# The second layer's experts in a two-layer kernel: four dense experts against tokens sent to their two experts in 35 tiles of 128 slots

## The chip, the cores and the metric

The kernel runs on one core of one Trainium2 chip. The metric is the device time of one execution in microseconds (us), as the median of several runs. Engines are called TensorE (PE in the rows, PEld for its weight loads), VectorE (DVE), ScalarE (ACT), GpSimd (POOL) and SyncE (SP); a "q" behind a name means what the engine's sequencer issues, such as DMA.

## The reference

Two layers work on x of shape (2, 1024, 128), all in float32. Each layer adds a gated attention and then a gated expert network, each of them on a normalised x. The change concerns the second layer's expert network and where its routing is worked out:

```python
logits = xf @ gate_w.T                       # 8 experts, of which the last 4 are masked out
weights = softmax(logits)
top_w, top_idx = top_k(weights, 2)
top_w = top_w / sum(top_w)                   # cw: the two weights of a token, zero elsewhere
h = silu(einsum('td,edh->teh', xf, w1)) * einsum('td,edh->teh', xf, w3)    # h is 704 wide
y = einsum('teh,ehd->ted', h, w2)
out = einsum('te,ted->td', cw, y)
x = x + gb * out
```

There are 2048 tokens, four live experts, and every token uses two of them. The attention before it is a linear attention with 16 heads of 32 and decay 0.99, written in chunks of 128 tokens. The first layer has an RWKV-style scan and 16 experts, of which each token uses one.

## The kernel before

The program is a row of phases, each with an instruction stream per engine, ordered by hand with semaphores: set-up, the first layer's scan (`rwkv_phase`), its experts (`expert_phase`), the second layer's attention (`hla_phase`) and its experts (`swiglu_phase`). The weights of the second layer are loaded during the scan.

The first layer's experts already work by dispatch, and are of use as a model. GpSimd scatters the 16 tiles of token rows into slots in DRAM with an indirect transfer each (L1012). SyncE reads from a list in SBUF which expert each tile of 128 slots has (`value_load`, eight at the head of each round), loads the weights (L971) and the rows (L975). The results go back through DRAM, and GpSimd gathers them (L1019). TensorE's matmuls there have fixed addresses.

The attention (`hla_phase`) takes, for each of the 8 chunks, 8 units (2 batches by 4 groups of 4 heads), one a step, so 64 steps and a few more to fill and drain. Steps are pipelined: step k projects unit k+2 (L1325 to L1327), transposes and multiplies k+1 (L1340, L1341, L1363), and finishes k and k-2 (L1383 to L1426). VectorE has three instructions a step: the decay on the chunk's matrix (L1498), the state (L1501) and the masking of 128x1536 products (L1507), for which TensorE waits at the next step's products. Twice a chunk the output projection runs (L1350), ScalarE copies it (L1474), and GpSimd scales it and adds it to x (L1523, L1526). The first and the last chunk are written out; the six between are a loop, so TensorE returns to the loop's head five times.

The experts (`swiglu_phase`) begin when all of x is there. A prologue normalises the 16 tiles (L1730 to L1742, L1799, L1801), transposes them (L1630), works out logits (L1624), the top two and a table of weights per token and expert. Then four groups of 512 tokens run through all four experts. GpSimd multiplies the rows by each expert's weight (L1813), TensorE transposes them (L1647), and each of 22 units per group (a slice of 128 of the hidden width) has two up matmuls of 512 columns with the weights as the stationary side (L1661, the tails in L1663), a silu on ScalarE (L1718), a product on VectorE (L1786) and a down matmul into one accumulator (L1671). Every f32 matmul shows as two instructions, a transpose as one. At a group's end the output is transposed back (L1690), gated (L1790), added to x (L1829) and stored by SyncE (L1837).

## Time and profile before

| | |
|---|---|
| median of three runs | 977.8 us (977.65 to 982.03) |
| the profiled execution, its time | 981.48 us |
| its span in the profile | 979.7 us |
| TensorE busy with matmuls | 778.6 us, 79% of the span |
| VectorE, ScalarE, GpSimd busy | 418.8, 296.4 and 185.3 us |
| mean granted TensorE clock | 0.852 of full speed |

Busy time of an engine is the time in which at least one of its instructions runs. Matmuls are pipelined, so a matmul's own duration is longer than its pitch (the distance between starts), and the pitch is what counts in a stream. A granted clock of 1.00 is 2.4 GHz, of 0.50 is 1.2 GHz. An idle time in brackets stands before an instruction, with what ended it; "issue" means that nothing seen in the profile did.

### The profile page before, as it was taken

The page shows a single profiled execution, that of the slowest core. Times are in us where ns is not written, and L with a number is a line of the kernel's source. Part 1 is how long each engine was busy: PE and PEld are TensorE (multiplying, and loading weights), DVE is VectorE, ACT ScalarE, POOL GpSimd, SP SyncE. Part 2 cuts the span into 40 slices and gives each one's busy share as a digit, 9 for nine tenths or more (in the row PEclk, how much of TensorE's full clock was granted, in tenths as well). Part 3 has the DMA queues.
Part 4 walks back from the last instruction along what each step waited for, and adds up shares of the span by engine and source line. Part 5 has one row for each costly group of instructions (what it writes and reads, how often), then busy time and mean ns, then how long its engine had stood idle before and what let it go on. Part 6 is the DMA issues. An engine that isn't in the chain of part 4 may idle for free. (4 is left out here: it accounts for less than half of the span.)

```text
span 979.7 us, 25889 instructions
## 1 busy us (share of the span) xinstructions
PE 778.6 (79%) x10310; PEld 544.4 (56%) x10310; DVE 418.8 (43%) x1142; ACT 296.4 (30%) x903; POOL 185.3 (19%) x285
## 2 busy tenths in 40 slices
PE   3777777754238608998898988999459999999997
PEld 3455555533238506887787877887334444444442
DVE  4367777772413264444443444444522222222221
ACT  0243333330014304443333433343122222222221
POOL 1244444432230170000000000000221010110100
PEclk9587777765559858999999999999659999999999
DMA  4600000002147510000000000000000000000000
GB/s 139 220 3 2 0 0 0 0 2 86 34 144 232 156 38 2 4 3 4 3 4 3 3 4 3 4 3 3 1 0 1 0 12 0 11 0 0 11 0 11
DMA packets 27297, 28.11 MB, mean 29 GB/s; under 512 B 3201, under 2 KB 20289, under 8 KB 27201
## 3 DMA queue, kind: packets, MB, share of 16 engines
q1 hardware_dynamic: 26176, 24.58, 8.1%
q0 software_dynamic: 1024, 2.10, 0.7%
q8 instruction: 79, 1.29, 0.6%
q14 instruction: 18, 0.14, 0.0%
HBM read 20.38 MB, written 6.29 MB: 27 GB/s over the span
## 5 line engine op out<-in xcount | busy, mean ns | idle before, releaser
L1507 DVE TENSOR_TENSOR h_masked<-quad,const 128x1536 f32<-128x1536 f32 (+2 forms) x66 | 112.8, 1709 | 143.3 <-PE quad L1369 136.5
L1661 PE MATMUL quad<-f_xg,moe_w 128*128 128x512 f32 x320 | 152.3, 601 | 0.8 <-ACT f_xg L1706 0.8
L1786 DVE TENSOR_TENSOR f_h<-f_sa,quad 128x512 f32<-128x512 f32 x88 | 60.6, 688 | 181.0 <-PE quad L1661 164.6
L1661 PEld LDWEIGHTS quad<-f_xg,moe_w 128*128 128x128 f32 x320 | 60.2, 193 | 69.8 <-issue 69.1
L1718 ACT ACTIVATE f_sa<-quad 128x512 f32<-128x512 f32 x88 | 52.5, 597 | 143.7 <-PE quad L1661 126.6
L1671 PE MATMUL bank<-f_h,moe_w 128*128 128x512 f32 x160 | 82.5, 597 | 0.0
L1523 POOL TENSOR_TENSOR h_added<-h_added,mod_row 128x128 f32<-128x128 f32 x16 | 7.3, 455 | 285.2 <-ACT h_added L1474 285.2
L1671 PEld LDWEIGHTS bank<-f_h,moe_w 128*128 128x128 f32 x160 | 29.7, 190 | 40.9 <-issue 40.9
L1478 ACT ACTIVATE h_gT<-bank 128x128 f32<-128x128 f32 x64 | 17.7, 277 | 113.4 <-PE bank L1412 111.9
L1363 PE MATMUL quad<-h_qk 32*128 32x128 f32 x1024 | 49.6, 311 | 0.0
L1325 PE MATMUL pair<-h_hT,hla_wq 128*128 128x128 f32 x128 | 32.1, 334 | 20.4 <-issue 16.6
L1454 ACT ACTIVATE h_qk<-pair 128x256 f32<-128x256 f32 x64 | 24.5, 383 | 71.6 <-PE pair L1327 71.6
L1363 PEld LDWEIGHTS quad<-h_qk 32*128 32x128 f32 x1024 | 36.8, 197 | 10.8 <-issue 8.8
L633 POOL TENSOR_TENSOR kl<-kl,tot 128x128 f32<-128x128 f32 x56 | 26.9, 481 | 60.7 <-DVE tot L543 28.7
L1813 POOL TENSOR_TENSOR g_hs<-g_h_all,g_cw 128x512 f32 (+1 forms) x20 | 20.6, 1040 | 93.0 <-PE pair L1647 71.6
L1829 POOL TENSOR_TENSOR x_sb<-x_sb,f_gated 128x512 f32 x4 | 5.1, 1266 | 155.9 <-DVE f_gated L1790 155.9
L1325 PEld LDWEIGHTS pair<-h_hT,hla_wq 128*128 128x128 f32 x128 | 19.6, 193 | 24.8 <-issue 18.3
L1498 DVE TENSOR_TENSOR h_aT<-bank,const 128x128 f32<-128x128 f32 x64 | 18.7, 292 | 30.1 <-PE bank L1426 27.4
L711 ACT ACTIVATE rl<-rl 128x128 f32<-128x128 f32 x56 | 17.3, 308 | 44.6 <-DVE rl L544 28.4
L1383 PE MATMUL bank<-h_qk,h_state 32*32 32x128 f32 x512 | 28.1, 290 | 0.0
L757 PE MATMUL quad<-lh,b_pad 128*128 128x256 f32 x64 | 27.2, 598 | 0.7 <-ACT lh L666 0.7
L1019 POOL DMA_INDIRECT e_yt<-slots_out,slot_of_token x16 | 15.7, 978 | 62.8 <-DMA slots_out<-e_yg 58.3
(287 smaller groups left out, 1685.8 us busy)
## 6 DMA issues: line engine op xcount, KB each, us to landing
e_w<-in_experts_dram SPq DMA_DIRECT2D x32, 257.5 KB
moe_w<-in_moe_w_dram SPq DMA_DIRECT2D x2, 1408.0 KB, 9.2
slots_in<-zero SPq DMA_DIRECT2D x4, 512.0 KB, 4.0
e_xg<-slots_in SPq DMA_DIRECT2D x8, 256.0 KB, 3.0
slots_out<-e_yg SPq DMA_DIRECT2D x8, 256.0 KB, 4.8
moe_w<-in_moe_w_dram SPq DMA_DIRECT2D x4, 320.0 KB, 7.0
x_sb<-in_L_attn_x_dram SPq DMA_DIRECT2D x2, 512.0 KB, 8.5
out_dram<-x_sb SPq DMA_DIRECT2D x4, 256.0 KB, 2.3
```

What stands on the lines that cost most here:

```text
L633: pool.tensor_tensor(halves(kl[m + 1], m)[:, :, 0], halves(kl[m], m)[:, :, 0], per(tot[m], m)[:, :, 1:2].to_broadcast([P, N >> (m + 1), 1 ...
L757: mm = pe.matmul(bank[2 + f // 2][:, f % 2 * N:(f % 2 + 1) * N], b_pad[:, f, :], lh[:, :], start=True, stop=True)
L1325: pe.matmul(proj[:, 0:P], W["q"][:, cols], hT[b][:, :], start=True, stop=True)
L1363: last = pe.matmul(quad[:, h, a * P:(a + 1) * P], qk[q][head(h), 1 - a, :], qk[q][head(h), a, :], start=True, stop=True, tile_position=(h ...
L1383: pe.matmul(left[head(h), 0:P], states[k][head(h), 2 * D:3 * D], qk[k][head(h), 1, :], start=True, stop=False, tile_position=(h * D, h * D ...
L1454: act.activation(qk[q][:, :, :], proj[:, 0:2 * P].rearrange("p (k n) -> p k n", k=2), ACT.Copy).then_inc(s_qkv, 1)
L1507: dve.tensor_tensor(masked[k % 4][:, :, a * P:z * P], quad[:, :, a * P:z * P], cst("causal")[:, None, a * P:z * P].to_broadcast([P, HPG, ( ...
L1661: return pe.matmul(dst[:, :], w[:, e, f * P:(f + 1) * P], src(e), start=True, stop=True)
L1671: pe.matmul(acc[b][:, :], w, hh[n % 2][:, :], start=(n == 0), stop=(n == U - 1))\
L1718: act.activation(sa[n % 2][:, :], up_a[n % 2][:, :], ACT.Silu).then_inc(s_sa, 1)
L1786: dve.tensor_tensor(hh[n % 2][:, :], sa[n % 2][:, :], up_b[n % 2][:, :], ALU.mult)\
L1813: pool.tensor_tensor(hs[k % 2][:, :, :], h_all[:, bass.ds(at + k, 1), :].to_broadcast([P, E, C]), cw[:, 0, bass.ds(at + k, 1), :].rearrang ...
```

## The change

The two phases become one, `layer1_phase`. Four things change.

1. **Routing during the attention.** As soon as a chunk's x is there, the steps of the next two chunks carry its routing: statistics (step 3), centring (4), normalising (5), logits as products on GpSimd and sums on VectorE (7), the top two (0), ranks by two small matmuls on TensorE (1), slots and weights (2). The attention's second chunk is now written out too, so the loop has five turns and four returns.
2. **Dispatch.** A payload row has 132 numbers: the normalised row, the token's number, its weight and its batch. GpSimd sends each tile's rows to the slots of its first and of its second expert: four indirect transfers a chunk. The slots in DRAM are filled with blank rows during the scan. SyncE writes x into an accumulator in DRAM as it becomes ready.
3. **The expert loop.** 35 tiles of 128 slots (the most that four experts can need), in 7 rounds of 5, the last one written out. TensorE reads from SBUF which expert each tile has, six `value_load`s at a round's head (five in the last), and takes the weights by that register. Now the tokens are the stationary side and the weights move: three up matmuls of 512, 512 and 384 columns hold w1 and w3 side by side, the hidden tile is transposed (4 + 2 transposes) and six down matmuls of 128 columns make the rows. One tile's parts are interleaved with the next one's.
4. **Results.** VectorE multiplies a row by weight and gate, and GpSimd adds the tile into the accumulator with an accumulating indirect transfer, each after the one before has landed, since two tiles can hold the same token. At the end SyncE copies the accumulator, 1 MB, from DRAM to the output.

```diff
+CAP1 = BATCH * SEQ
+TILES1 = 2 * BATCH * SEQ // P + E1_LIVE - 1
+SLOTS1 = E1_LIVE * CAP1 + (E1_LIVE - 1) * P
+PAY = C + 4
+S_W2 = 7 + E1_LIVE
...
+        W2 = {"up": sb("moe_up", [P, E1_LIVE, 2 * F1]), "w2": sb("moe_w2", [P, E1_LIVE, FULL1, C]),
+              "w2_tail": sb("moe_w2_tail", [TAIL1, E1_LIVE, C])}
+        blank = sb("blank", [P, PAY])
+        s_fill = sem("s_fill1")
+        t["moe1_slots"] = nc.dram_tensor("moe1_slots", (SLOTS1, PAY), F32, kind="Internal").ap()
+        t["moe1_acc"] = nc.dram_tensor("moe1_acc", (BATCH * SEQ + P, C), F32, kind="Internal").ap()
...
-                hla_phase(nc, x_bc, mod_row, quad, bank, pair, cst, hT_all, W1, s_w1)
-        with nc.cleanup_on_exit():
-            swiglu_phase(nc, t, x_sb, eps_pow, sbw[:, 1], mod_row, bank, pair, cst, W2, s_w2, out)
+                layer1_phase(nc, t, x_sb, x_bc, eps_pow, sbw[:, 1], mod_row, quad, bank, pair, cst, hT_all, W1, s_w1,
+                             W2, s_w2, s_fill, blank, out)
...
+            sp.dma_start(t["moe1_slots"].rearrange("(q p) n -> p q n", p=P),
+                         blank[:, None, :].to_broadcast([P, SLOTS1 // P, PAY])).then_inc(s_fill, 16)
...
+            for i in range(2):
                 for k in range(PER):
-                    step(n + 1, k)
+                    step(i, k)
+            with eng.Fori(0, CHUNKS - 3) as n:
+                for k in range(PER):
+                    step(n + 2, k)
...
+        def routed(i, k, at):
+            if k % PER != at:
+                return None
+            m = i + k // PER - (1 if at >= 3 else 2)
+            return m if not isinstance(m, int) or m >= 0 else None
...
+            pe.wait_ge(s_gate, 16)
+            for e in range(E):
+                last = pe.matmul(left[:, e * C:(e + 1) * C], gate[:, e:e + 1].to_broadcast([P, P]), cst("ident"),
+                                 start=True, stop=True)
+            last.then_inc(s_grow, 1)
+            pe.wait_ge(s_growc, 1)
...
+            def rank(m, first):
+                pe.wait_ge(r_ohs, m + 1)
+                pe.wait_ge(r_cum, m * 2 + 1)
+                pe.nop(nofuse=True)
+                pe.matmul(right[:, 232:240], cst("before"), ohs[:, :, :].rearrange("p b e -> p (b e)"), start=first,
+                          stop=False, skip_group_check=True)
+                pe.matmul(right[:, 232:240], cst("ones"), cum[:, :, :].rearrange("p b e -> p (b e)"), start=False,
+                          stop=True, skip_group_check=True).then_inc(r_rank, 1)
...
+            def ups(i, k, u, e):
+                if u == 0:
+                    pe.wait_ge(f_xT, tile(i, k) + 1)
+                pe.wait_ge(f_hh, tile(i, k) * 3 + (u + 1))
+                pe.nop(nofuse=True)
+                w = 2 * WIDTH[u]
+                pe.matmul(up[u][:, 0:w], xT[k][:, :],
+                          W2["up"][:, bass.ds(e, 1), u * 4 * P:u * 4 * P + w].rearrange("p e n -> p (e n)"),
+                          start=True, stop=True).then_inc(f_up, 1)
+            def turn_most(i, k):
+                pe.wait_ge(f_hh, tile(i, k) * 3 + 5)
+                pe.wait_ge(f_mostc, tile(i, k) + 1)
+                for f in range(4):
+                    last = pe.transpose(most[:, f * P:(f + 1) * P], hh[k][:, f * P:(f + 1) * P], cst("ident"))
+                last.then_inc(f_most, 1)
+            def turn_rest(i, k):
+                pe.wait_ge(f_hh, tile(i, k) * 3 + 6)
+                pe.wait_ge(f_restc, tile(i, k) + 1)
+                for f in range(2):
+                    last = pe.transpose(rest[:, f * P:(f + 1) * P], hh[k][:, (4 + f) * P:(5 + f) * P], cst("ident"))
+                last.then_inc(f_rest, 1)
+            def down(i, k, e):
+                pe.wait_ge(f_mostc, tile(i, k) + 2)
+                pe.wait_ge(f_restc, tile(i, k) + 2)
+                pe.wait_ge(f_y, tile(i, k) + (1 if k else 2))
+                pe.nop(nofuse=True)
+                for f in range(FULL1):
+                    pe.matmul(acc[k % 2], hidT[k][:, f * P:(f + 1) * P],
+                              W2["w2"][:, bass.ds(e, 1), f, :].rearrange("p e n -> p (e n)"), start=(f == 0),
+                              stop=False)
+                pe.matmul(acc[k % 2], hidT[k][0:TAIL1, FULL1 * P:(FULL1 + 1) * P],
+                          W2["w2_tail"][:, bass.ds(e, 1), :].rearrange("p e n -> p (e n)"), start=False,
+                          stop=True).then_inc(f_down, 1)
+            def expert(n):
+                return pe.value_load(expert_of[0:1, bass.ds(n, 1)], min_val=0, max_val=E - 1)
+            def round_(i, last):
+                es = [expert(tile(i, k)) for k in range(U if last else U + 1)]
+                for k in R:
+                    j, q = (i, k + 1) if k + 1 < U else (i + 1, 0)
+                    more = not last or k + 1 < U
+                    ups(i, k, 2, es[k])
+                    turn_most(i, k)
+                    if not last or k + 2 < U:
+                        turn(*((i, k + 2) if k + 2 < U else (i + 1, k + 2 - U)))
+                    if more:
+                        ups(j, q, 0, es[k + 1])
+                    turn_rest(i, k)
+                    if more:
+                        ups(j, q, 1, es[k + 1])
+                    down(i, k, es[k])
+            turn(0, 0)
+            first = expert(0)
+            ups(0, 0, 0, first)
+            turn(0, 1)
+            ups(0, 0, 1, first)
+            with pe.Fori(0, ROUNDS - 1) as i:
+                round_(i, False)
+            round_(ROUNDS - 1, True)
...
+            def weigh(m):
+                act.wait_ge(r_gap, m + 1)
+                act.activation(eg[:, :], gap[:, :], ACT.Exp).then_inc(r_eg, 1)
...
+            def top2(m):
+                dve.wait_ge(r_lg, m * 2 + 2)
+                dve.nop(nofuse=True)
+                for b in range(BATCH):
+                    dve.max(mx[:, b, :], lg[:, b, :]).then_inc(r_mx, 1)
+                dve.wait_ge(r_mx, m * 2 + 2)
+                dve.nop(nofuse=True)
+                for b in range(BATCH):
+                    dve.max_index(idx[:, b, :], mx[:, b, :], lg[:, b, :]).then_inc(r_idx, 1)
+                dve.tensor_tensor(gap[:, :], mx[:, :, 1], mx[:, :, 0], ALU.subtract).then_inc(r_gap, 1)
+                dve.wait_ge(r_idx, m * 2 + 2)
+                dve.tensor_copy(idf[:, :, :], idx[:, :, 0:2]).then_inc(r_idf, 1)
+                dve.wait_ge(r_idf, m + 1)
+                dve.tensor_tensor(oh[:, :, :, :],
+                                  cst("iota16")[:, None, None, 0:E].to_broadcast([P, BATCH, 2, E]),
+                                  idf[:, :, :, None].to_broadcast([P, BATCH, 2, E]), ALU.is_equal).then_inc(r_oh, 1)
+                dve.wait_ge(r_oh, m + 1)
+                dve.tensor_tensor(ohs[:, :, :], oh[:, :, 0, :], oh[:, :, 1, :], ALU.add).then_inc(r_ohs, 1)
+                dve.wait_ge(r_ohs, m + 1)
+                dve.tensor_tensor(cum[:, 1, :], cum[:, 0, :], ohs[:, 0, :], ALU.add).then_inc(r_cum, 1)
...
+                m = routed(i, k, 2)
+                if m is not None:
+                    ranked(m)
                 if live(i, k, -3, LAST):
                     q = unit(i, k, -3)[1]
                     dve.scalar_tensor_tensor(out=states[q][:, :], in0=states[q][:, :], scalar=GAMMA ** P,
                                              in1=right[:, P:P + 3 * D], op0=ALU.mult, op1=ALU.add).then_inc(s_st, 1)
+                if m is not None:
+                    slots(m)
+                    weights(m)
+                for at, part in ((3, stats), (4, centre), (5, normalise), (7, logits), (0, top2)):
+                    m = routed(i, k, at)
+                    if m is not None:
+                        part(m)
...
+            def hidden(i, k, u):
+                dve.wait_ge(f_sa, (i * U + k) * 3 + (u + 1))
+                at, w = u * 2 * P, WIDTH[u]
+                dve.tensor_tensor(hh[k][:, at:at + w], sa[u][:, 0:w], up[u][:, w:2 * w], ALU.mult).then_inc(f_hh, 1)
+            def keep_rest(i, k):
+                dve.wait_ge(f_rest, i * U + (k + 1))
+                dve.tensor_copy(hidT[k][:, 4 * P:6 * P], rest).then_inc(f_restc, 1)
+            def result(i, k):
+                n = i * U + (k + 1)
+                dve.wait_ge(f_down, n)
+                dve.wait_ge(f_gs, n * 3)
+                if not isinstance(i, int) or i:
+                    dve.wait_ge(f_add, (i * U + (k + 1 - U)) * 16 + 16)
+                dve.scalar_tensor_tensor(out=yg[k][:, :], in0=acc[k % 2], scalar=xg[k][:, C + 1:C + 2],
+                                         in1=gsel[k][:, :], op0=ALU.mult, op1=ALU.mult).then_inc(f_y, 1)
+            def round_(i, last):
+                for k in R:
+                    hidden(i, k, 2)
+                    j, q = (i, k + 1) if k + 1 < U else (i + 1, 0)
+                    keep_rest(i, k)
+                    if not last or k + 1 < U:
+                        hidden(j, q, 0)
+                        hidden(j, q, 1)
+                    result(i, k)
...
+            def chunk(i, first=2, last=False):
+                if first >= 1:
+                    add(i - 1, 1)
+                if not last:
+                    pool.wait_ge(s_proj, i * PER + GROUPS)
+                    fetch(i + 1, 0)
+                if first >= 2:
+                    send(i - 2)
+                if first >= 1:
+                    deviation(i - 1)
+                    products(i - 1)
+                    payload(i - 1)
+                add(i, 0)
+                if not last:
+                    pool.wait_ge(s_proj, i * PER + 2 * GROUPS)
+                    fetch(i + 1, 1)
+            chunk(0, 0)
+            chunk(1, 1)
+            with pool.Fori(0, CHUNKS - 3) as n:
+                chunk(n + 2)
+            z = CHUNKS - 1
+            chunk(z, 2, True)
+            send(z - 1)
+            add(z, 1)
+            deviation(z)
+            payload(z)
+            send(z)
+            pool.wait_ge(r_sent, CHUNKS * 64)
+            pool.wait_ge(s_acc, 16 * TILES)
+            pool.wait_ge(s_table, 1)
...
+            def send(m):
+                pool.wait_ge(r_pay, m * 2 + 2)
+                pool.wait_ge(r_slot, m + 1)
+                pool.wait_ge(r_cw, m * 3 + 3)
+                pool.nop(nofuse=True)
+                for b in range(BATCH):
+                    for k in range(2):
+                        pool.indirect_dma_start(out=t["moe1_slots"], out_offset=bass.IndirectOffsetOnAxis(
+                            ap=slot[:, b * 2 + k:b * 2 + k + 1], axis=0), in_=pay[:, b, k, :], in_offset=None)\
+                            .then_inc(r_sent, 16)
...
+            def select(i, k):
+                pool.wait_ge(f_x[k], i * 16 + 16)
+                pool.nop(nofuse=True)
+                pool.tensor_copy(token_of[k][:, :], xg[k][:, C:C + 1]).then_inc(f_gs, 1)
+                pool.tensor_tensor(gsel[k][:, :], gdiff[:, :], xg[k][:, C + 2:C + 3].to_broadcast([P, C]),
+                                   ALU.mult).then_inc(f_gs, 1)
+                pool.wait_ge(f_gs, (i * U + k) * 3 + 2)
+                pool.tensor_tensor(gsel[k][:, :], gsel[k][:, :], mod_row[:, 1, 1, 0, :], ALU.add).then_inc(f_gs, 1)
+            def scatter(i, k):
+                n = i * U + (k + 1)
+                pool.wait_ge(f_gs, n * 3)
+                pool.wait_ge(f_y, n + 2)
+                pool.wait_ge(f_add, n * 16)
+                pool.nop(nofuse=True)
+                pool.indirect_dma_start(out=t["moe1_acc"], out_offset=bass.IndirectOffsetOnAxis(
+                    ap=token_of[k][:, 0:1], axis=0), in_=yg[k][:, :], in_offset=None, compute_op=ALU.add)\
+                    .then_inc(f_add, 16)
             with pool.Fori(0, ROUNDS) as i:
-                for b in range(BATCH):
-                    prepare(*following(i, b))
-                    pool.wait_ge(s_gated, group(i, b) + 3)
-                    xs = x_sb[:, bass.ds(i * TPG + b * CHUNKS, TPG), :]
-                    pool.tensor_tensor(xs, xs, gated[b][:, :, :], ALU.add).then_inc(s_x, 1)
+                for k in R:
+                    select(i, k)
+                    scatter(i, k)
+            pool.wait_ge(f_add, 16 * TILES1 + 16)
...
+            def rows_of(i):
+                return [sp.value_load(row_of[0:1, bass.ds(i * U + k, 1)], min_val=0, max_val=SLOTS1 - P) for k in R]
+            def load(k, row):
+                sp.dma_start(xg[k][:, :], t["moe1_slots"][bass.ds(row, P), :]).then_inc(f_x[k], 16)
+            for k, row in enumerate(rows_of(0)):
+                load(k, row)
+            with sp.Fori(0, ROUNDS - 1) as i:
+                following = rows_of(i + 1)
+                for k in R:
+                    sp.wait_ge(f_y, i * U + (k + 3))
+                    sp.nop(nofuse=True)
+                    load(k, following[k])
+            sp.wait_ge(f_add, 16 * TILES1 + 16)
+            whole = "(q r) n -> q (r n)"
+            sp.dma_start(out.rearrange("b s n -> (b s) n").rearrange(whole, q=P),
+                         t["moe1_acc"][0:BATCH * SEQ, :].rearrange(whole, q=P)).then_inc(f_out, 16)
+            sp.wait_ge(f_out, 16)
```

Not shown are the new constants, the layout of the weight loads (w1 and w3 in six transfers side by side), VectorE's table of 35 tiles worked out on one partition after the last chunk, and the small bodies of `stats`, `centre`, `normalise`, `logits`, `ranked`, `slots`, `weights` (13 VectorE instructions a chunk), `deviation`, `products` and `payload` (six on GpSimd), of which `products` has two of 128x512. ScalarE's and VectorE's waits in the expert loop follow TensorE's order.

## Rows read from the trace of the kernel before

**Rows 1.** Busy time by stretch: length, each engine (instructions), granted clock, DMA share, GB/s.

```profile
370.80:691.00 320.20, 298.35 (x7232) 259.65 (x7232) 141.20 (x194) 120.78 (x464) 21.62 (x48) 0.96 0.01 3
691.00:728.60 37.60, 14.63 (x64) 12.69 (x64) 18.55 (x124) 6.40 (x11) 11.30 (x15) 0.52 0.01 1
728.60:972.40 243.80, 241.52 (x636) 105.19 (x636) 62.63 (x91) 66.36 (x109) 20.91 (x22) 0.99 0.01 4
```

**Rows 2.** Timeline of TensorE in the expert loop: start us, us, engine, line, what.

```profile
746.15 1.88 PE L1661 MATMUL quad<-f_xg,moe_w 128*128 128x512 f32 x4
...
747.87 1.02 PE L1671 MATMUL bank<-f_h,moe_w 128*128 128x512 f32 x2
```

**Rows 3.** Timeline of TensorE in the first layer's experts, 128-column matmuls.

```profile
319.75 0.39 PE L1212 MATMUL bank<-const,e_w 128*128 128x128 f32 x2
319.97 0.61 PE L1209 MATMUL bank<-e_w,e_hid 128*128 128x128 f32 x4
```

**Rows 4.** Timeline of TensorE in an attention step, transposes.

```profile
588.02 0.27 PE L1341 MATMUL pair<-const,h_qk 128*128 128x128 f32 x1
588.12 0.27 PE L1345 MATMUL pair<-const,h_gT 128*128 128x128 f32 x1
```

**Rows 5.** Costliest groups, VectorE and ScalarE: busy and mean ns | idle before.

```profile
L1786 DVE TENSOR_TENSOR f_h<-f_sa,quad 128x512 f32<-128x512 f32 x88 | 60.6, 688 | 181.0 <-PE quad L1661 164.6
...
L1718 ACT ACTIVATE f_sa<-quad 128x512 f32<-128x512 f32 x88 | 52.5, 597 | 143.7 <-PE quad L1661 126.6
```

**Rows 6.** Timeline of VectorE and SyncE around the first layer's register loads.

```profile
260.91 0.17 DVE L1109 TENSOR_SCALAR expert_of_tile<-r_te 1x32 int32<-1x32 f32 x1
...
266.16 4.36 SPq L971 DMA_DIRECT2D e_w<-in_experts_dram  x8
...
298.35 0.41 SPq L979 DMA_DIRECT2D slots_out<-e_yg  x1
...
304.70 0.39 SPq L975 DMA_DIRECT2D e_xg<-slots_in  x1
```

**Rows 7.** Timeline of TensorE at a return of the attention loop.

```profile
449.54 0.48 PE L1325 MATMUL pair<-h_hT,hla_wq 128*128 128x128 f32 x2 [3.05 <-issue]
```

**Rows 8.** Busy time by stretch around the same return.

```profile
448.00:450.00 2.00, 0.46 (x4) 0.47 (x5) 0.00 (x0) 0.00 (x0) 0.00 (x0) 1.00 0.00 0
450.00:452.00 2.00, 2.00 (x20) 1.67 (x22) 0.00 (x0) 1.33 (x5) 0.00 (x0) 0.54 0.03 8
```

**Rows 9.** Timeline of ScalarE, the copy that comes twice a chunk.

```profile
421.94 0.38 ACT L1474 ACTIVATE h_added<-pair,const 128x128 f32<-128x128 f32 x1
...
439.88 0.38 ACT L1474 ACTIVATE h_added<-pair,const 128x128 f32<-128x128 f32 x1
...
462.48 0.38 ACT L1474 ACTIVATE h_added<-pair,const 128x128 f32<-128x128 f32 x1
```

**Rows 10.** Timeline of GpSimd and SyncE, last scatter and the load after it.

```profile
279.77 0.95 POOL L1012 DMA_INDIRECT slots_in<-h_all,slot_of_token  x1 [0.31 <-issue]
...
282.01 0.94 SPq L975 DMA_DIRECT2D e_xg<-slots_in  x2
```

**Rows 11.** DMA issues: count, KB each, median us from issue to landing.

```profile
e_xg<-slots_in SPq DMA_DIRECT2D x8, 256.0 KB, 3.0
...
x_sb<-in_L_attn_x_dram SPq DMA_DIRECT2D x2, 512.0 KB, 8.5
...
e_yt<-slots_out,slot_of_token POOLq DMA_INDIRECT x16, 2.5
...
g_gate<-in_gate_cols_dram SPq DMA_DIRECT2D x1, 2.0 KB, 1.6
```

**Rows 12.** Timeline of an attention step, VectorE and TensorE's next products.

```profile
589.35 1.76 DVE L1507 TENSOR_TENSOR h_masked<-quad,const 128x1536 f32<-128x1536 f32 x1 [1.61 <-PE quad L1369]
...
592.59 0.73 PE L1363 MATMUL quad<-h_qk 32*128 32x128 f32 x16
```

**Rows 13.** Timeline of GpSimd, the last addition to x.

```profile
690.30 0.45 POOL L1526 TENSOR_TENSOR x_sb<-x_sb,h_added 128x128 f32<-128x128 f32 x1
```

551 lines of the change are left out of this document (282 added, 269 removed).

## The prediction

> **What bounds the kernel now.** I read first the busy time by stage. The second layer's attention runs from 370.8 to 691.0 us and its experts from 728.6 to 972.4 us, with a routing prologue of 37.6 us between. In both long stages TensorE is busy nearly throughout (298 of 320 us, 241.5 of 243.8 us), and no other engine reaches half the stage [rows 1]. So an instruction added to another engine costs nothing while it fits beside TensorE, and whatever shortens or stretches TensorE's stream moves the end. Second, the timeline gives the pitch of that stream: four passes of 512 columns take 1.72 us, 0.43 us each, two to a matmul [rows 2]; an f32 matmul of 128 columns takes 0.22 us (two passes) [rows 3], a transpose 0.10 us, say 0.11 [rows 4]. Third, I looked at what happens when TensorE's sequencer has nothing to hand over, at a loop's return and at register loads, since the new loop has these.
>
> **The expert loop.** Removed: 243.8 us. Each of 35 tiles has three up matmuls (512, 512 and 384 columns: 0.86 + 0.86 + 0.65 = 2.37), seven transposes (0.77) and six down matmuls (1.32): 4.46 us. That is 156 us in all; the halved count of experts is partly spent on transposes and on 35 tiles where 32 would be full. I take 4.6 us for small gaps at the four no-operations that wait. Do the others keep up? ScalarE has three silus and two copies: an activation or copy of 256 columns is near 0.4 us and one of 512 is 0.60 on the rows of VectorE and ScalarE scale [rows 5], in all about 2.0 us; VectorE has three products, a copy and the result, about 1.7. Both are below half, and each hand-over (silu, product, back to a transpose) has an up matmul of 0.86 us over it. So they cost nothing; without that cover each hand-over would show about 1 us.
>
> Every matmul on the experts' weights now takes its address from a register. No TensorE row shows one. Below: nothing (SyncE's register-addressed loads already go out at 4.36 / 8 = 0.55 us, near the 0.39 of an ordinary issue). Above: 0.15 us for each of nine, 1.4 us a tile, 47 us. A dispatch of this size hides under passes of 0.43 us, so I take nothing and keep 20 us for the range.
>
> **Register loads, at every round's head.** TensorE reads six expert numbers into registers before each round of five tiles. SyncE shows what such a load costs: the expert list is written at 261.1, and the first weight load goes out at 266.16, after eight of them: 0.63 each. In the loop, 298.76 to 304.70 is 5.94 for eight, 0.74 each with the loop's return [rows 6]. Six cost 3.8 to 4.4 us; the matmuls already handed over (the last down group, 1.32 us) cover about 0.9. I take a hole of 3.5 us. The nearest TensorE row is the attention loop's own return: idle 3.05 us before the first matmul of a turn [rows 7], and then a stretch at a granted clock of 0.54, which is the 1.2 GHz level against 1.00 before [rows 8]. Its whole price is that a half chunk takes 22.60 instead of 17.94 us: 4.66 [rows 9]. So each hole is 3.5 + 1.3 = 4.8 us, six of them 29 us. Bounds: nothing, if TensorE's loads are quick; 6 us each if they also wait for the array. In the Trainium skill, "DMA: Bandwidth & Descriptors", section "Latency and other measured facts", a tensor load has a floor of about 600 ns; by it the six would take 3.6 us, 0.2 us less a hole than by the rows. The Trainium skill, "TensorE: Matmul & The Clock Gate", section "HAM oscillation", adds that a loop which stops between bursts of matmuls is throttled again in each turn; that speaks against this change, and rows 8 agree at a hole of this size. Were the clock to hold, the six holes would cost 21 us.
>
> So the loop is 35 x 4.6 = 161, less 1.7 (no next tile in the last one), plus 29, plus 1.3 for a cold start: 189.6 us.
>
> **The scatter-add.** GpSimd sends each tile's rows with an accumulating indirect transfer, and each waits for the one before to land. The nearest row is a plain scatter: issued at 279.77, all landed when SyncE moves at 282.01, 2.24 us [rows 10]. If the read of the old rows adds a whole gather (2.5 us [rows 11]), that is 4.7, about 5 with the wait. GpSimd's own work (select about 1.4, issue 0.95 + 0.31 = 1.26 [rows 10]) fits in 2.8. A round averages 5.56 us a tile (4.6 plus 4.8 / 5), and results are five deep. I take 3.5 us and no cost; it begins to cost at 5.56. The row loads (3.0 us to land [rows 11]) are issued three tiles ahead, 9 us of cover.
>
> **The attention stage.** Moved in: statistics, normalising, logits, top two, ranks, slots and sends, one or two parts per step. TensorE's added work is two tiny matmuls per chunk, 0.22 each, with waits about 0.6: 7 x 0.6 = 4 us. VectorE has in each step 1.61 us idle before the big masking product [rows 12], and TensorE wants that product about 1.5 us after its end, so 3 us fit into a step. The largest part (top two, ten small instructions of about 0.2) is 1.8, logits 1.4. Queued behind them is only the mask. GpSimd's four sends per chunk take 4 x 1.26 = 5 us of a half chunk, and the normalising that waits for them comes two steps later. So no stall; without this cover 1 to 2 us per chunk, up to 15. One chunk more is written outside the loop: one return less, -4.7. Ahead of the stage, loading gate rows (1.6 us to land, four matmuls, a copy) delays TensorE by 3.5. The last steps lose 1. Sum +4.
>
> **Between attention and loop.** The send of chunk 6 now stands on GpSimd ahead of the last addition, which ended at 690.75 [rows 13]: four issues, +4.6. The last x is ready at 690.75 + 4 + 4.6 = 699.4. From there: statistics 0.9, deviation 1.2, normalising 0.6, products 1.4 (VectorE 0.69 each [rows 5]), logits 1.4, top two 1.5, ranks 0.9, slots and weights 1.4: 9.3. Then four sends and their landing, 6.3; SyncE's five register loads 3.1 and the first row load 2.9; transpose and copy 0.9; and before the loop's first instruction the first six register loads, of which 4.8 us count. Sum 27.3. The loop begins at 726.7, where its predecessor began at 728.6: the removed 37.6 us are spent again on latency.
>
> **The tail.** Before, 972.4 to 979.7, 7.3 us. Now: result 0.5, last scatter about 3.5, and a DRAM to DRAM copy of 1 MB, nearest row 8.5 us for 1 MB in two loads at the start [rows 11]; I take 7.5 with its issue, 0.9 to the end: 12.4. Bounds 8 and 16.
>
> **Sum.** 726.7 + 189.6 + 12.4 = 928.7, against 979.7: 51 us less. The profiled execution took 981.5 us, 1.8 outside the span and 3.7 above the median of 977.8; 977.8 - 51 = **927 us**.
>
> **Rivals.** (a) TensorE's register loads hide under queued matmuls or are quick. Against: SyncE's rows; for: no TensorE row. Loop -29, start -4: 894 us. (b) Tiles of 5.2 to 5.8 us, by register addresses or hand-overs that miss their cover: +21 to +42, 948 to 969. (c) The routing work in the attention stalls TensorE, by a late send or mask: +15 to +30, 942 to 957. (d) The other side: the serial chain of scatter-adds sets the pace. It costs from 5.56 us a link, equals the time before at 5.56 + 51 / 35 = 7.0, and at 8 us a link gives 927 + 35 x 2.44 = 1012. For it: each transfer waits for the last, and no row shows an accumulating one; against: the plain scatter lands in 2.24 us.
>
> **How the numbers follow.** Forecast 0.53 (910 to 942), (a) 0.17, (b) 0.14, (c) 0.07, (d) 0.09, of which 0.06 is slower. The predicted time is that of the forecast, 927. The range 888 to 965 takes in (a) and most of (b) and (c). A measurement tells about 0.5% (5 us): faster 0.92, same 0.02, slower 0.06.
>
> **What would show it.** Right: seven holes of 3 to 4 us on TensorE at the rounds' heads, with the granted clock near 0.5 behind each; a pitch near 4.6 us within a round; attention steps of unchanged length; first up matmul near 722. Wrong: GpSimd's scatter waiting for the transfer before it while TensorE waits for VectorE's result; masking products that start late in the steps with logits or top two; holes missing.

## The result, and the profile after

The changed kernel takes **1000.4 us** (median of 4, 997.9 to 1004.1), the kernel before 979.9 beside it: ratio 1.021, 95% interval 1.016 to 1.026. So it is slower, by about 2%; 927 us was forecast, range 888 to 965. The profiled execution has a span of 1002.3 us.

The same marks that the forecast was built on, in us from the start of the span:

| mark | before | forecast | after | added to the miss |
|---|---|---|---|---|
| last row of the first layer's scan (ScalarE, zT) | 229.5 | 229.5 | 239.8 | +10.3 |
| first half-chunk copy of the attention (ScalarE, h_added) | 404.0 | 407.5 | 420.3 | +2.5 |
| last half-chunk copy | 689.3 | 693.3 | 751.1 | +45.0 |
| last addition to x ends | 690.8 | 699.4 | 757.9 | +0.7 |
| first up matmul | | 721.9 | 780.8 | +0.4 |
| last down matmul ends | 972.4 | 916.3 | 990.9 | +15.7 |
| end of the span | 979.7 | 928.7 | 1002.3 | -1.0 |

Busy time by stretch of the changed kernel (length, PE, PEld, DVE, ACT and POOL busy with counts, granted clock, DMA share, GB/s); it answers to [rows 1]:

```profile
383.60:752.00 368.40, 327.84 (x7268) 279.24 (x7268) 174.59 (x382) 129.13 (x477) 73.62 (x114) 0.91 0.04 10
752.00:780.70 28.70, 2.06 (x7) 1.61 (x7) 9.81 (x48) 1.97 (x4) 11.98 (x17) 0.53 0.11 31
780.70:991.00 210.30, 184.15 (x874) 117.87 (x874) 65.56 (x175) 64.99 (x174) 88.23 (x137) 0.94 0.16 21
991.00:1002.30 11.30, 0.00 (x0) 0.00 (x0) 0.27 (x1) 0.00 (x0) 1.58 (x1) 0.58 0.33 99
```

The expert loop did become shorter, 210 us for 244. But the attention, whose matmuls are the same but for two small ones a chunk, went from 320 to 368 us. TensorE idles 40.6 us of it for 21.9, and the granted clock is 0.91 for 0.96. No other engine is near full there either. So the stage didn't get a new bound; it got holes. The list of TensorE's waits in that stage says of which kind (engine, tile, line <- what ended the wait: us in total, times, longest):

```profile
PE pair L1430 <- issue: 16.1, 5, 3.6
PE pair L1431 <- issue: 10.1, 4, 2.7
PE bank L1494 <- issue: 6.4, 11, 1.0
PE bank L1488 <- issue: 4.8, 14, 0.4
PE bank L1409 <- DMA g_gate<-in_gate_cols_dram: 3.5, 1, 3.5
```

No wait for a mask, a rank or a send is among them. "Issue" is a wait for nothing that the profile shows. Before, the only wait for issue was the one of the first line (16.6 us, 5 times). Three places are to be seen. First, a return of the loop, timeline of TensorE, answering to [rows 7]:

```profile
504.06 0.24 PE L1546 MATMUL bank<-h_vt,h_kqt 128*32 128x32 f32 x8
507.87 0.50 PE L1430 MATMUL pair<-h_hT,hla_wq 128*128 128x128 f32 x2 [3.56 <-issue]
511.02 0.79 PE L1431 MATMUL pair<-h_hT,hla_wk 128*128 128x128 f32 x2 [2.65 <-issue]
```

There is a second stop of 2.65 us after the first two matmuls of a turn, where [rows 7] had one stop and then went on. Second, the half chunk in which GpSimd issues its four sends (527.0 to 531.9), TensorE and GpSimd:

```profile
529.67 0.96 POOL L1978 DMA_INDIRECT moe_slots<-g_pay,g_slot  x1 [0.30 <-issue]
529.73 0.37 PE L1488 MATMUL bank<-h_qk,h_state 32*32 32x128 f32 x2 [0.34 <-issue]
...
530.47 0.42 PE L1488 MATMUL bank<-h_qk,h_state 32*32 32x128 f32 x5 [0.36 <-issue]
...
530.94 0.96 POOL L1978 DMA_INDIRECT moe_slots<-g_pay,g_slot  x1 [0.30 <-issue]
531.18 0.27 PE L1488 MATMUL bank<-h_qk,h_state 32*32 32x128 f32 x1 [0.29 <-issue]
```

and the stretches around it:

```profile
528.00:530.00 2.00, 1.66 (x29) 1.21 (x26) 1.09 (x6) 0.00 (x0) 1.39 (x3) 1.00 0.20 57
530.00:532.00 2.00, 1.01 (x11) 0.42 (x11) 0.00 (x0) 1.34 (x5) 1.62 (x3) 1.00 0.17 53
532.00:534.00 2.00, 1.54 (x21) 1.08 (x20) 1.15 (x1) 0.00 (x0) 0.91 (x2) 0.52 0.10 34
534.00:536.00 2.00, 2.00 (x42) 1.77 (x44) 0.61 (x1) 0.32 (x2) 0.00 (x0) 0.50 0.00 0
```

I call it the stutter: TensorE gets its matmuls in crumbs for some 4 us, of which it idles about 1.8, and the granted clock then falls from 1.00 to 0.50 (1.2 GHz) for some 7 more (it is 0.77 in 538 to 540 us and 1.00 from 540 on). What both cost is read from ScalarE's copy, as in [rows 9]:

```profile
497.70 0.38 ACT L1685 ACTIVATE h_added<-pair,const 128x128 f32<-128x128 f32 x1
...
524.69 0.38 ACT L1685 ACTIVATE h_added<-pair,const 128x128 f32<-128x128 f32 x1
...
548.89 0.38 ACT L1685 ACTIVATE h_added<-pair,const 128x128 f32<-128x128 f32 x1
```

The half chunk with the return takes 26.99 us (22.60 before), the one with the sends 24.20 (17.94 before). Third, the scan, which the change doesn't touch. At 51.4 us TensorE stops 2.0 us before line 820, and where the kernel before has its clock back at about 51 us (0.92 in 50 to 55 us, 1.00 in 55 to 60), this one stays at the half level until 68 us:

```profile
50.00:55.00 5.00, 3.56 (x36) 2.88 (x37) 2.16 (x8) 1.02 (x4) 1.26 (x3) 0.50 1.23 274
55.00:60.00 5.00, 5.00 (x31) 2.73 (x30) 1.95 (x4) 0.00 (x0) 2.58 (x5) 0.50 0.30 67
```

The 274 GB/s are the fill of the slot rows, which is new.

In the expert loop, the end of a round and the head of the next, timeline of TensorE:

```profile
809.11 1.34 PE L1618 MATMUL bank<-moe_w,h_masked 128*128 x10
810.39 0.48 PE L1621 MATMUL bank<-moe_w_tail,h_masked 64*128 x2
815.19 1.46 PE L1594 MATMUL quad<-moe_up,f_xT 128*128 x2 [4.31 <-issue]
```

The holes forecast at 3.5 us are there, with 4.1 to 4.3 us at five heads of rounds and 2.6 at the last, which has five loads and no return. At the first of the seven heads TensorE idles only 1.43 us. The pitch inside a round is 4.925 us (the tail's down matmul starts at 790.69, 795.61, 800.54, 805.46), not 4.6.

### The profile page after: what moved, and what is told of

Same layout as the page of the kernel before. It is cut to its first block, busy times and chain, and to the rows that moved or that the text cites. A ratio compares the mean times of both kernels' runs of the same rounds, so it can differ in the third digit from the quotient of the medians.

```text
span 1002.3 us, 28133 instructions
## 1 busy us (share of the span) xinstructions
PE 747.4 (75%) x10523; PEld 571.3 (57%) x10524; DVE 447.4 (45%) x1347; ACT 298.7 (30%) x974; POOL 307.9 (31%) x473
## 3 DMA queue, kind: packets, MB, share of 16 engines
q8 instruction: 81, 1.33, 0.6%
## 4 chain that ended last, share of the span: by engine, by line
PE 51%; issue 7%; POOL 1%; DMA 1%; DVE 1%; ACT 0%; SPq 0%; POOLq 0%; DVEq 0%; PEldq 0%
PE quad L1594 10%; PE quad L1468 5%; PE bank L1618 4%; PE bank L1494 3%; PE pair L1430 3%; PE bank L1488 3%; PE bank L1521 2%; PE pair L1431 2%; PE quad L1474 2%; PE quad L1602 2%; PE pair L1432 2%; PE bank L1505 2%; PE bank L1538 2%; PE bank L1526 2%; PE bank L1529 2%
## 5 line engine op out<-in xcount | busy, mean ns | idle before, releaser
L1594 PE MATMUL quad<-moe_up,f_xT 128*128 x210 | 111.6, 615 | 25.5 <-issue 23.5
L2045 POOL DMA_INDIRECT moe_acc<-f_y,f_token x35 | 55.4, 1582 | 120.5 <-DVE f_y L1916 120.5
L1904 DVE TENSOR_TENSOR h_masked<-f_sa,quad 128x256 f32<-128x256 f32 (+1 forms) x105 | 41.5, 395 | 85.0 <-ACT f_sa L1713 85.0
L1713 ACT ACTIVATE f_sa<-quad 128x256 f32<-128x256 f32 (+1 forms) x105 | 38.4, 365 | 137.0 <-PE quad L1594 136.2
L1618 PEld LDWEIGHTS bank<-moe_w,h_masked 128*128 128x128 f32 x350 | 41.8, 191 | 22.1 <-issue 22.1
L1594 PEld LDWEIGHTS quad<-moe_up,f_xT 128*128 128x128 f32 x210 | 33.8, 202 | 32.5 <-issue 29.1
L1618 PE MATMUL bank<-moe_w,h_masked 128*128 x350 | 47.0, 281 | 0.7 <-DVE h_masked L1908 0.7
L1430 PE MATMUL pair<-h_hT,hla_wq 128*128 128x128 f32 x128 | 33.7, 348 | 16.9 <-issue 16.1
L1978 POOL DMA_INDIRECT moe_slots<-g_pay,g_slot x32 | 31.9, 997 | 25.9 <-DVE g_pay L1822 16.6
L1494 PE MATMUL bank<-h_aT,h_state 32*32 32x128 f32 x512 | 30.5, 278 | 7.0 <-issue 6.4
L1431 PE MATMUL pair<-h_hT,hla_wk 128*128 128x128 f32 x128 | 27.9, 303 | 10.1 <-issue 10.1
```

Source lines behind the costliest of these rows:

```text
L1430: pe.matmul(proj[:, 0:P], W["q"][:, cols], hT[b][:, :], start=True, stop=True)
L1431: pe.matmul(proj[:, P:2 * P], W["k"][:, cols], hT[b][:, :], start=True, stop=True)
L1494: pe.matmul(left[head(h), P:2 * P], states[q][head(h), part * D:(part + 1) * D], of[head(h), :], start=(part == 2 and not live(i, k, 0)), ...
L1594: pe.matmul(up[u][:, 0:w], xT[k][:, :], W2["up"][:, bass.ds(e, 1), u * 4 * P:u * 4 * P + w].rearrange("p e n -> p (e n)"), start=True, sto ...
L1618: pe.matmul(acc[k % 2], hidT[k][:, f * P:(f + 1) * P], W2["w2"][:, bass.ds(e, 1), f, :].rearrange("p e n -> p (e n)"), start=(f == 0), sto ...
L1713: act.activation(sa[u][:, 0:WIDTH[u]], up[u][:, 0:WIDTH[u]], ACT.Silu).then_inc(f_sa, 1)
```

## The experiments

Times are medians; "before" is the kernel before on the same chip in the same group. It took 980.5, 981.9, 982.8, 980.3 and 980.6 us in the five groups.

### Group 1: four single edits

Fill in the middle of the scan:

```diff
+            sp.wait_ge(s_gT, 5)
+            sp.nop(nofuse=True)
             sp.dma_start(t["moe1_slots"].rearrange("(q p) n -> p q n", p=P), ...
```

> The 4.4 MB fill of the slot rows waits until the scan is at its fifth chunk; nothing else differs from the changed kernel. Theory A (TensorE's instructions arrive late because the fill's transfers, 274 GB/s at 50 us, are ahead of them): the 2.0 us stop before TensorE's line 820 at 51.4 us is gone, the clock rises to 1.00 at about 50 us as before the change (55 to 60 us: 1.00, not 0.50), the last scan row is back from 239.8 near 229.5, and the whole is 8 to 11 us shorter, 990 to 993, unless the fill stops TensorE at its new place. Rival B (the weights, now loaded in 11 transfers with shorter rows in place of 10, or the code's place, are the cause): no change, 1000 to 1003, the stop stays at 51 us.

No sends:

```diff
-                for b in range(BATCH):
-                    for k in range(2):
-                        pool.indirect_dma_start(out=t["moe1_slots"], ...).then_inc(r_sent, 16)
+                pool.sem_inc(r_sent, 64)
```

> GpSimd issues none of the 32 sends (all slot rows keep their blank content, so the experts work on zero rows and add to the spare rows; the output holds x before the experts); routing, masks and rank matmuls stay. Theory A (the sends delay TensorE's instructions): TensorE's waits for issue at lines 1488 and 1494 (4.8 + 6.4 us) are gone, and with them the half clock behind them; the half chunks without a loop return go from 22.8 to 24.2 us back to 17.9 to 18.6, in all 20 to 30 us less, and 5 us less behind the last x where GpSimd is no longer held up; whole about 970 to 978. Rival C (the routing work on VectorE and GpSimd holds TensorE up): 997 to 1003, the half chunks stay. Both: the 3.6 us return and the 2.65 us second stop at lines 1430 and 1431 stay, since no send runs beside them.

x written to the sum table after the attention:

```diff
-            with sp.Fori(0, CHUNKS) as i:
-                for b in range(BATCH): ...
+            for b in range(BATCH):
+                sp.wait_ge(s_x, CHUNKS * BATCH + (b + 1))
+                sp.dma_start(rows[b], x_bc[:, b, :, :]).then_inc(s_acc, 16)
```

> SyncE writes x to the sum table in two transfers of 512 KB when the last x is ready, in place of 16 of 64 KB during the attention. If the 64 KB writes take part in delaying TensorE's instructions (one is issued at 526.5 us, just ahead of the stutter at 528.7 to 533.4): the stutter shrinks by up to half, 5 to 15 us less, 985 to 995. If only the sends do: within 3 us of the changed kernel, 998 to 1003. The two transfers themselves (8.5 us for such a one at the start of the kernel) lie beside the 27 us between the last x and the expert loop; if they don't, up to 5 us more.

TensorE's attention written out:

```diff
-            steps(pe, step)
+            step(0, -2)
+            step(0, -1)
+            for i in range(CHUNKS - 1):
+                for k in range(PER):
+                    step(i, k)
+            for k in range(PER + 3):
+                step(CHUNKS - 1, k)
```

> TensorE's attention steps are written out for all 8 chunks; the other engines keep their loops. The four loop returns of TensorE cost 3.56 + 2.65 us of stop and some 1.7 us at half clock behind each. Theory A (code comes by transfers, a jump back starts them anew): all four stops of both kinds are gone, 4 x (6.2 + 1.7) = 32 us less, about 969; the stutter beside the sends stays. Rival D (the stop at a return is a wait for another engine's return, the loop registers or a barrier of all engines): a stop of 1 to 3.5 us stays at the same place, 985 to 1000. Rival E (written-out code is always fetched too slowly at full rate): the stutter spreads over all chunks, no gain or a loss, 1000 to 1020.

Measured: fill late 963.4 (ratio to before 0.981, 0.976 to 0.986); no sends 960.0; x after 972.4 (0.988, 0.984 to 0.993); written out 936.6 (0.954, 0.949 to 0.960). All gained far more than I gave them against the first run of the changed kernel: the late fill 37 us for 8 to 11, no sends 40 for 22 to 30, x written after 28 for at most 15, written out 64 for 32. In **none** of the four was there a stutter, though three of them send: the half chunks with sends took 17.94 us. That three unrelated edits should each cure it is hard to believe; the next groups have a control. What the group does show: the late fill is 9.0 us below x written after, which has everything else of the changed kernel. With it the stop at line 820 is gone and the clock is 1.00 from 50 us on:

```profile
50.00:55.00 5.00, 5.00 (x39) 3.22 (x38) 3.80 (x12) 1.09 (x5) 3.51 (x7) 1.00 0.00 0
```

and with TensorE written out, all returns with both their stops are gone (last less first half-chunk copy: 264.8 us, where the loop of the kernel before takes 285.3).

### Group 2: a control, two paddings, spread register loads

> The changed kernel once more, word for word, as the control of this group. Three edits that have nothing to do with each other (the fill later, the x rows written later, TensorE's steps written out) each took away the whole stutter of TensorE beside the sends, in two of them with the sends still running. Theory F (the stutter belongs to this one build: where its instructions or rings lie): it is there again, lines 1488 and 1494 wait 11 us for issue, 998 to 1004. Theory G (it belonged to the chip or the moment of the first run): it is gone here, the loop chunk takes 44.5 us in place of 51.2, about 972 (1000 less 5 chunks of some 5 to 6).

Empty instructions on SyncE, and on TensorE:

```diff
+            for n in range(2):
+                sp.nop(nofuse=True)
             for n in "qkv":
                 sp.dma_start(W1[n][:, :], ...
```

> Two empty instructions on SyncE ahead of its weight loads, nothing else, so that later code lies 128 bytes further and nothing that is computed or moved changes. Theory F: if placement decides, the stutter can go: about 972, with the second stop and the fill's 10 us still there; if the edits of the first group took it away by what they do, it stays, 998 to 1004. Theory G: the same time as the control.

```diff
+            for n in range(32):
+                pe.nop(nofuse=True)
             pe.wait_ge(s_gate, 16)
```

> 32 empty instructions on TensorE ahead of the attention, where it waits 3.5 us for the gate columns anyway, so that its loop begins 2 KB later in its code. The second stop (2.65 us after two of the loop's first matmuls, in every return of every kernel that has the loop) is the edge of a block of code right behind the loop's first instructions: moved by 2 KB it is gone and the next block comes while the first runs: 4 x 2.65 = 10.6 us less than the control, and some of the half clock. Rival: the second stop is a property of a return with so many engines in loops: it stays, same time as the control within 3 us.

One register load ahead of each tile (in a round's code on TensorE):

```diff
-                es = [expert(tile(i, k)) for k in range(U if last else U + 1)]
+                es = [expert(tile(i, 0))]
                 for k in R:
...
+                    if more:
+                        es.append(expert(tile(i, k + 1)))
```

> TensorE's register loads of the round's experts stand one ahead of each tile (two ahead of the first) in place of six ahead of the round. If TensorE's matmuls before a load go on while the load is under way (the 1.3 us of downs ahead of it would cover one load of 0.6 to 0.7): 5 holes of 4.2 fall to about 1.5 and the others vanish, 5 x 2.7 + 1.3 of clock each, 15 to 22 us less than the control. If a load stops TensorE fully: the same sum in smaller pieces, each tile some 0.6 longer, and only the half clock behind the long holes is saved: 0 to 8 us less.

Measured: 1000.6, 1003.1, 997.8 and 974.1 us. The stutter is in all four, as in the first run, so the two empty instructions on SyncE do nothing, and the first group's lack of it seems to lie with its chip. The 32 on TensorE left the second stop (2.9 us). The spread loads are worth 26.5 us, more than I expected: the holes, where two loads still stand in a row at a round's head, are 1.3 us at most (6.4 in six), and the tiles between them keep their pitch of 4.92, so a single load that follows 1.3 us of down matmuls is hidden.

### Group 3: the sends and the chip

> The changed kernel once more, as the control of this group. The first group (fill late, no sends, x rows after, TensorE written out) ran on one chip and had no stutter in any kernel; the second (the changed kernel, two kernels with empty instructions, spread loads) ran on another and had it in all four. Theory G (the stutter belongs to the chip): it is in all kernels of this group or in none. Theory A (it belongs to the edit): here and not in the two of this group with the fill late or without sends. Time 998 to 1004 with it, about 970 without.

> The kernel with the fill in the middle of the scan again, beside a control on the same chip. Theory G: the control less 8 to 10 us (the scan's part alone), its stutter as in the control. Theory A: no stutter whatever the control has, 960 to 966, 35 to 40 us below the control. It would mean that a transfer that ended at 56 us decides over TensorE's supply at 500 us, which I hold for unlikely (1 in 4).

> The kernel without the 32 sends again (what it leaves out is as before), beside a control on the same chip. If the control has the stutter and this one not: the sends are one half of its cause, the chip the other; 30 us or more below the control, 957 to 962. If both have it: the sends have no part. If neither has it: this kernel is 5 to 15 us below the control, by the last send that is not waited for.

> Fill in the middle of the scan, TensorE's attention steps written out, register loads spread: the three edits that gained singly (each of them correct). If they add (37 less 28 of stutter, that is 9, and 936.6 for the second, and 26 for the third): 936.6 - 9 - 26 = 902. If the stutter is there on this chip in written-out code too: 25 to 30 more, 925 to 935.

Measured: 1004.4, 996.9, 958.5 and 931.8 us. The control has the stutter, the late fill has it too (so it was never the fill), and the kernel without sends has none. The waits of TensorE there, for issue alone:

```profile
PE pair L1430 <- issue: 16.0, 5, 3.7
PE pair L1431 <- issue: 9.3, 4, 2.7
...
PE pair L820 <- issue: 1.7, 1, 1.7
```

From the first to the last half-chunk copy the control takes 329.7 us and this one 298.5. So on a chip that shows it, the sends cost 31 us of the attention. On the chip of group 1 the nearest pair (fill late with sends, 297.2; fill early without, 298.1) does not differ by more than 1 us. The three edits together (931.8) keep the stutter: written-out code doesn't cure it, the half chunks with sends take 23.0 to 24.3.

The late fill is 7.5 us below its control. The last zT is at 226.3 to 231.7 in the four kernels with the late fill and at 229.9 to 239.8 in all the others of the change, 235 in the mean; so the early fill costs some 2 to 10 us and 6 in the mean, not always the 10.3 of the first profile. These are single executions, and the mark moves by itself: in three profiles of the kernel before and its variants, which have no fill, it is at 227.5, 229.5 and 235.1. The two differences of whole times, 9.0 and 7.5 us, are the better measure.

### Group 4: transfers or their issue; register addresses; before written out

Plain sends, by SyncE:

```diff
+            def sends(m):
+                sp.wait_ge(r_pay, m * 2 + 2)
...
+                        sp.dma_start(t["moe1_slots"][bass.ds(m * 4 * P + (b * 2 + k) * P, P), :], pay[:, b, k, :])\
+                            .then_inc(r_sent, 16)
```

> The 32 sends go as plain transfers of the same 128 rows of 528 bytes, issued by SyncE at the same point of the chunk, to rows that follow each other in place of the routed ones (so the experts work on rows in another order and the sums go wrong); GpSimd issues none. Theory H (the transfers themselves hold up the blocks of TensorE's instructions): the half chunks with sends stay at 22.8 to 24.2 us where the chip shows the stutter at all (see the 12-nop kernel of this group), whole 995 to 1004. Theory I (it is what GpSimd does to issue an indirect send: its descriptors): they fall to 17.9, TensorE waits for issue at lines 1488 and 1494 under 1 us in all, whole 958 to 965.

> 12 empty instructions on TensorE ahead of the attention, 768 bytes of code. With 32 of them (2 KB) the second stop of each loop return stayed at 2.9 us; if it is an edge of a block of 2 KB or a divisor of it that lies 4 to 6 instructions behind the loop's start, 12 move it: the second stop is gone or moved, 10 us less for the stops and up to 10 more for the half clock behind them, 980 to 990. If it stays (2.1 to 2.9 us after the first two matmuls, 996 to 1004), no edge of code explains it. This kernel is also the group's control for the stutter.

Fixed experts:

```diff
-                return pe.value_load(expert_of[0:1, bass.ds(n, 1)], min_val=0, max_val=E - 1)
+                return n
...
-                es = [expert(tile(i, k)) for k in range(U if last else U + 1)]
+                es = [k % E for k in range(U + 1)]
```

> Every tile uses a fixed expert (0, 1, 2, 3, 0 by its place in the round; the sums go wrong, the work is the same): no register loads on TensorE and no addresses from registers. Against the kernel with spread loads, whose tile takes what the loads leave (group of the control: 1000.6 and 974.1), this prices register addresses: the forecast took 0 for them and bounded them at 1.4 us a tile. From the trace (five downs 1.28 us for 1.10, the tail's 0.41 for 0.22, ups 2.47 for 2.37): 0.3 to 0.47 a tile, so a pitch of 4.46 to 4.6 in place of 4.93 and holes of 1.1 at the returns: 35 x 0.4 + 6 x 3.2 = 33 us less than the changed kernel, 965 to 970. If the addresses cost nothing, the pitch stays at 4.9 and 19 us less, 981.

> The kernel before, with TensorE's attention steps written out for all chunks. Its five returns cost 4.66 us each: 23.3 us less, 957, since nothing else of it is touched and no sends run beside it. The changed kernel gained more from the same edit, because its returns cost 9.3 us. If the gain is the same 23, the difference that the change makes once both are rid of returns is 936.6 to 957.

Measured: plain sends 962.4, 12 empty instructions 999.3, fixed experts 959.3, before written out 956.4 (0.975, 0.969 to 0.982). The second and third, with GpSimd's sends, have the stutter (10.0 and 11.6 us of waits at lines 1488 and 1494); the plain sends have none. Timeline of SyncE and TensorE there:

```profile
517.40 2.64 SPq L2067 DMA_DIRECT2D moe_slots<-g_pay  x4
...
518.94 0.42 PE L1488 MATMUL bank<-h_qk,h_state 32*32 32x128 f32 x8
...
519.18 0.40 PE L1494 MATMUL bank<-h_aT,h_state 32*32 32x128 f32 x8
```

Line 1488's eight matmuls go in one piece right beside the four transfers. The bytes are the same, so it is the way in which GpSimd issues them (with two reservations: these rows land one behind the other, the routed ones scattered; and no kernel lets GpSimd issue plain transfers, so the engine and the indirection are not told apart). The Trainium skill, "DMA: Bandwidth & Descriptors", section "Terms", says that the software path writes its descriptors to rings in SBUF, while the hardware path feeds the DMA engines directly. The difference between these two kernels agrees with that as the place to look; no run shows the rings.

Fixed experts: within the loop there is no hole left at all, and the pitch is 4.858 (tails at 779.42, 784.28, 789.14):

```profile
775.00:940.00 165.00, 164.92 (x849) 110.79 (x847) 63.93 (x170) 63.34 (x170) 85.69 (x132) 1.00 0.20 26
```

So a return of this short loop costs nothing, the whole hole is register loads, and the nine register addresses of a tile cost 0.067 us together, 2.3 in all. Written out, the kernel before has 17.94 in every half chunk up to the last two and gains 24. The 12 empty instructions left the second stop where it was.

### Group 5: the cut of the loop, and pairs of sends

The kernel before with the loop cut as the change cuts it:

```diff
-            for k in range(PER):
-                step(0, k)
-            with eng.Fori(0, CHUNKS - 2) as n:
+            for i in range(2):
+                for k in range(PER):
+                    step(i, k)
+            with eng.Fori(0, CHUNKS - 3) as n:
                 for k in range(PER):
-                    step(n + 1, k)
+                    step(n + 2, k)
```

> The kernel before with its attention loop on TensorE, ScalarE and VectorE cut as the change cuts it: two chunks written out ahead of it, five turns in place of six, nothing routed. The forecast took 4.7 us off for the return that is saved: 975.5. If the second stop of 2.1 to 2.9 us comes from that cut (where the loop lies, what precedes it), it shows in all four returns here: 4 x 4.9 - 4.7 = 15 us more, 995. If it comes from what the routing put into the loops (longer bodies on VectorE, ScalarE and GpSimd, which return at the same time), it is absent and the time is 973 to 978.

The three edits, and the sends in pairs:

```diff
                 if first >= 2:
-                    send(i - 2)
+                    send(i - 2, (0,))
                 if first >= 1:
                     deviation(i - 1)
+                if first >= 2:
+                    pool.wait_ge(s_left, i * PER + 4)
+                    send(i - 2, (1,))
```

> The three edits together (931.8 us, clock stutter beside the sends still in it, 5.1 to 6.3 us for each half chunk with four sends) and the four sends of a chunk in two pairs, one at the third step, one when TensorE has done the third step, so that its supply can catch up between them. If what a send costs is its own 0.35 to 0.9 us of stops and the half clock comes only after four in a row: 7 x (3 to 4) = 20 to 28 us less, 904 to 912. If each pair still brings the half clock: no gain, 930 to 936. If the chip is one without the stutter: 900 to 905, as it would be for the four in a row. Loss possible where VectorE waits for the later pair at the fifth step: up to 1 us a chunk.

Measured: the cut 988.7 (1.007, 1.004 to 1.010), the pairs **899.4** (0.915, 0.912 to 0.918). The cut alone, without any routing, makes a return dearer, and the kernel 8 us slower than before (15 had been expected of a second stop as in the changed kernel). Timeline of TensorE at one of its returns:

```profile
535.34 0.79 PE L1326 MATMUL pair<-h_hT,hla_wq 128*128 128x128 f32 x2 [3.36 <-issue]
...
538.54 1.24 PE L1364 MATMUL quad<-h_qk 32*128 32x128 f32 x16 [0.92 <-issue]
```

and of ScalarE:

```profile
507.43 0.38 ACT L1475 ACTIVATE h_added<-pair,const 128x128 f32<-128x128 f32 x1
...
525.37 0.38 ACT L1475 ACTIVATE h_added<-pair,const 128x128 f32<-128x128 f32 x1
...
551.45 0.38 ACT L1475 ACTIVATE h_added<-pair,const 128x128 f32<-128x128 f32 x1
```

There is again a second stop, shorter (0.8 to 0.9 us) and some matmuls later, and behind it the clock stays at the half level for 9 us, to 544 us. The stretches there:

```profile
541.00:543.00 2.00, 2.00 (x41) 1.51 (x36) 1.03 (x1) 0.00 (x0) 0.00 (x0) 0.50 0.00 0
543.00:545.00 2.00, 2.00 (x42) 1.87 (x35) 0.45 (x2) 0.45 (x2) 0.00 (x0) 0.63 0.04 8
```

In the kernel before, the stretch that follows those of [rows 8] has the clock back after 4 us:

```profile
453.00:455.00 2.00, 2.00 (x64) 1.75 (x60) 1.69 (x1) 0.00 (x0) 0.00 (x0) 0.86 0.03 8
```

The half chunk with a return takes 26.1 to 26.5: 8.1 to 8.5 us a return, 33.3 for four, where the five of before cost 24.6. The changed kernel's four cost 33.7 (group 3, no sends). So the cut by itself brings a return to the changed kernel's price, though its second stop is shorter and lies elsewhere; that the two sums are so near each other may be chance.

The kernel with pairs has no stutter: every half chunk takes 17.94 or 18.6, but for the last two, which are shorter in every kernel. Its stretches: the first layer to 380, attention, what lies between, expert loop, tail:

```profile
380.00:676.00 296.00, 293.68 (x7254) 256.01 (x7254) 174.89 (x382) 127.36 (x475) 73.17 (x111) 0.99 0.04 12
676.00:702.00 26.00, 1.58 (x6) 1.43 (x6) 9.82 (x48) 1.69 (x3) 11.07 (x14) 0.55 0.07 24
702.00:890.00 188.00, 176.09 (x875) 113.44 (x875) 65.82 (x175) 65.37 (x175) 90.43 (x140) 0.98 0.19 25
```

But no kernel of this group sent four in a row, so whether the pairs did it or this chip shows no stutter is not told apart.

## Why the prediction was wrong

**The step that failed is "So no stall", in the attention stage, with "one return less, -4.7" beside it.** The sum for the stage's chunks came out 45.0 us short. I went through every engine that the new work stands on and through who waits for whom, and all of that held: no mask, rank or send was late, and the rank matmuls cost 0.68 a chunk for the 0.6 forecast. The loss came on another path. Beside GpSimd's four indirect sends TensorE, which waits for none of them, gets its work in crumbs for 4 us, and the half clock follows: +31 to 32 us, shown by leaving them out and by sending plainly. Four of the five groups' chips could be judged, three with it (and the first run's), one without. And the returns went from 4.9 to 8.4 us each: +13.8 against the forecast, shown by the cut alone. The rest is -1, the microsecond that the last steps were to lose.

**The gate rows, +2.5.** The delay forecast at 3.5 us is 4.8: from the first layer's last transposes to the attention's first matmul it was 365.14 to 372.02 us and is 375.98 to 387.62. The wait for the rows alone is 3.5; their four matmuls and the copy come on top, and the 3.1 us that TensorE waited there before fall away. The first layer adds 0.6, and a half clock that lasts one step longer adds 0.7. No rank matmul runs that early.

**The return taken as a constant.** I priced a return from [rows 9] and took one off. It is not a constant: five of 4.9 became four of 8.4 when one more chunk was written out ahead of the loop. Why the second stop lies where it does is open. What is known: it is in every kernel with the cut loop, it goes with the loop, and 768 bytes or 2 KB of code ahead of the loop don't move it. The changed kernel's page has a DMA queue called "instruction" with 81 packets and 1.33 MB, so 16 KB each; 19 of them come in 500 to 600 us, some 10 for a turn, and one in 800 to 900 us, where the loops are short. That they carry TensorE's instructions is inferred from these counts. Two of them lie in the return shown above:

```profile
GB/s 0 0 0 0 92 0 0 0 0 0 0 0 0 0 0 0 0 0 0 0 0 0 0 0 92 0 0 0 0 0 0 0 0 0 0 0 0 0 0 0
q8 instruction: 2, 0.03, 2.3%
```

The first line is 504.0 to 511.1 us in 40 slices, so the packets move at 504.8 and 508.3 us, each near the start of one of the two stops (504.3 and 508.4). By the Trainium skill, "Advanced Engine Details and Errata", section "ISA Cache", TensorE holds 128 KB in lines of 16 KB, 256 instructions. Ten packets for each turn agree with a body that is loaded anew every time. The size that this section states doesn't say why: written out, the kernel before needs 44 packets for six chunks, 7.3 each, which is less than eight lines. That "issue" in these places means instructions that come late fits all runs, but is argued and not shown.

**The scan, taken as untouched.** The fill (4.4 MB, 20 us) was costed at nothing without a sentence on it. With it TensorE stops for 2 us just where the clock would have risen, and without it neither happens: +10.3 in this profile, 7.5 and 9.0 us of the whole time in the two comparisons, each within one chip.

**The expert loop, +15.7.** Mechanism right, sizes off. The pitch: "4.6 us for small gaps" measured 4.925, 11.4 us over 35 tiles. "I take nothing" for register addresses was nearly right: 0.067 a tile for all nine, all of it in the five down matmuls (1.28 us, 809.11 to 810.39, and 1.21 with fixed addresses, 778.21 to 779.42). The other 0.26 is in the matmuls themselves, which come to 4.86 with fixed addresses, not 4.46: the tail's down matmul takes 0.42 to the next start where 0.22 was taken, the up matmul of 384 columns 0.75 for 0.65, the five down matmuls 1.21 for 1.10. The holes came out right as a sum, and that is luck: five cost 5.9 us each by the round (30.53 us less five tiles) and not 4.8, since TensorE idles 4.1 to 4.3 us and not 3.5, but the last costs 2.6 and the first about 1, so that the seven cost 34.0 (210.1 us of loop, less 173.8 with fixed experts, less 2.3) where 33.8 was forecast. The remaining 4 us are the slow first tile and the loop's two ends, which with fixed experts take 3.8 us beyond 35 tiles; the forecast had them at -0.4. Rival (a), loads hidden under queued matmuls, is false for six in a row and true for one at a time, and the loads one at a time are worth 26.5 us.

**Right as forecast:** last x to first up matmul 22.9 us (22.5), the tail 11.4 (12.4), no cost from the scatter-add: GpSimd waits 120.5 us for results, issues a scatter-add in 1.58 us, and it lands 3.3 us after its issue. Rival (d) never came near. Rival (c) named the right stage with the wrong cause and half the size: it looked for late sends and masks, and had +15 to +30.

**Sum:** 928.7 + 10.3 + 2.5 + 45.0 + 0.7 + 0.4 + 15.7 - 1.0 = 1002.3. The change's own idea, half the expert work, did pay in its place: with returns, fill and loads mended it stands at 899.4 (no stutter) or 931.8 (with it), and the kernel before with its returns mended at 956.4. On the chip without the stutter the changed kernel itself was not run; its nearest there, x written after, is 1.2% faster than before (0.984 to 0.993), so the sign of the change may hang on the chip.

## What to carry to other kernels

An engine that runs a long body at full rate can be stopped by what no list of waits names: here new indirect sends by GpSimd, a large fill and another cut of the loop stopped TensorE where no semaphore joins them (its supply of instructions is the likely link, and not shown). Such an edit needs its own term in the sum, with the price of the clock behind it. A long loop body on TensorE was worth writing out (956.4 for 980.3 us in the kernel before, 936.6 for 972.4 in the changed one, x written after, on the same chip), and register loads on TensorE belong one by one behind queued matmuls. And a difference between two kernels is read only beside a control on the same chip: three single edits that still send seemed to "cure" here what their chip does not show.

## What the hardware did that I had not expected

- Beside four indirect sends by GpSimd of 128 rows of 528 bytes (0.96 us issue each) TensorE stops in pieces of 0.3 to 1.0 us spread over some 4 us, which with the half clock behind them cost 5 to 6 us a time; the same rows by plain transfers from SyncE cost nothing (17.94 us a half chunk). On one chip the indirect ones cost nothing either (17.94).
- A TensorE loop return is 4.9 us in one cut of the loop and 8.4 in another; a return of the short expert loop (a turn is 5 tiles, 125 matmul rows) costs nothing with fixed experts.
- Behind a return whose second stop was only 0.9 us the clock stayed at the 1.2 GHz level for 9 us; behind a return without a second stop it came back after 4. That the second stop is the reason is not tested by itself.
- Six register loads in a row on TensorE, with the return, leave it idle 4.1 to 4.3 us, five without the return 2.6, one behind 1.3 us of queued matmuls nothing. Nine addresses from registers cost 0.067 us a tile.
- A scatter with addition lands 3.3 us after its issue (median of 35), near the 3.5 assumed, and its issue takes 1.58 us where one without addition takes 0.96.
